# Another order of the events in a round of the wedge-score stage

## The reference

```python
Q = (Q_input @ Wq_w.T + Wq_b).reshape(b, sq, H, dk).transpose(0, 2, 1, 3)
Kh = K.reshape(b, sk, H, dk).transpose(0, 2, 1, 3)        # K = V = the context
gen = x @ proj_w.T + proj_b                                # _psi, for Q and for K
A, Bg, Th = gen[..., 0:8], gen[..., 8:16], clip(gen[..., 16:24], -8, 8)
psi_real, psi_imag = A * exp(Th) + Bg * cos(Th), Bg * sin(Th)
...
gram = qn2[..., :, None] * kn2[..., None, :]
wedge = sqrt(max(gram - tensor**2 - spinor**2, 0) + 1e-6)
hodge = sqrt(qn2 + 1e-6)[..., :, None] * sqrt(kn2 + 1e-6)[..., None, :]
scores = (geo_w[0]*wedge + geo_w[1]*tensor + geo_w[2]*spinor + geo_w[3]*hodge) / 4 / temperature
out = softmax(scores) @ Vh  -> reshape -> @ Wo_w.T + Wo_b
```

## Time and profile before

| | |
|---|---|
| median of 3 runs | 3064.28 us (3058.69 to 3073.77) |
| profiled execution: time, span | 3060.05 us, 3058.3 us |
| busy share of the span: TensorE, VectorE, ScalarE, GpSimd | 83%, 54%, 45%, 10% |
| mean granted clock of TensorE | 0.905 |
| the stage psi | about 2148 to 2782 us of the span |

### The profile page before, as it was taken

The page is one execution under the profiler, slowest core; times in us unless marked ns, Lnnn a source line. Parts: engine busy times, 40 slices in busy tenths (PEclk is TensorE's granted clock), DMA queues, the critical chain, the costliest instruction groups (busy, mean ns, idle before and its releaser), DMA issues. The chain is left out here.

```text
span 3058.3 us, 31620 instructions
## 1 busy us (share of the span) xinstructions
PE 2547.7 (83%) x11456; PEld 1497.1 (49%) x11456; DVE 1638.0 (54%) x3416; ACT 1386.3 (45%) x1989; POOL 319.9 (10%) x299
## 2 busy tenths in 40 slices
PE   5888888875888888879997688897588888887998
PEld 3555556552333333355454455565344445444555
DVE  4566555624666666716444587877555555541222
ACT  2333333311655555532222656553377777772221
POOL 0010001000000000000276000000211111000000
PEclk7899888967999998979898799998799999998999
DMA  2000000005333332240146221211300001001000
GB/s 72 7 14 14 14 14 14 7 7 153 57 65 63 63 64 55 46 150 0 35 72 104 94 70 42 84 42 42 101 7 28 28 28 35 14 14 62 14 21 21
DMA packets 113394, 140.81 MB, mean 46 GB/s; under 512 B 22004, under 2 KB 96004, under 8 KB 113240
## 3 DMA queue, kind: packets, MB, share of 16 engines
q1 hardware_dynamic: 98888, 123.97, 14.9%
q0 software_dynamic: 11904, 14.69, 3.0%
q10 hardware_dynamic: 2448, 0.14, 0.1%
HBM read 77.89 MB, written 35.39 MB: 37 GB/s over the span
## 5 line engine op out<-in xcount | busy, mean ns | idle before, releaser
L950 DVE TENSOR_REDUCE xattn_tops<-region 128x2 f32<-128x1024 f32 x256 | 306.3, 1220 | 126.0 <-PE region L734 125.9
L887 ACT ACTIVATE xattn_probs<-region 128x1024 f32<-128x1024 f32 x256 | 256.4, 1022 | 125.8 <-PE region L723 124.5
L2088 PE MATMUL region<-psi_fT 128*128 128x512 f32 x512 | 247.2, 622 | 24.7 <-DVE psi_low L2364 15.2
L122 PE MATMUL region<-gla_xT,weights_even 128*128 128x512 f32 (+1 forms) x416 | 206.4, 649 | 30.6 <-ACT gla_xT L214 30.6
L723 PE MATMUL region<-xattn_qs,xattn_ks 49*128 49x512 f32 x512 | 126.4, 495 | 61.8 <-DVE xattn_tops L950 31.4
L122 PE MATMUL region<-mamba_xT,weights_odd 128*128 128x512 f32 x320 | 157.6, 641 | 3.2 <-DVE mamba_xh L1927 3.2
L2088 PEld LDWEIGHTS region<-psi_fT 128*128 128x128 f32 x512 | 93.8, 196 | 135.2 <-issue 101.9
L122 PEld LDWEIGHTS region<-gla_xT,weights_even 128*128 128x128 f32 (+1 forms) x416 | 78.0, 196 | 144.5 <-issue 109.5
L131 PE MATMUL region<-weights_even,gla_work 128*128 128x256 f32 x512 | 123.4, 403 | 26.0 <-ACT gla_work L484 24.7
L752 PE MATMUL region<-xattn_probs,xattn_va 128*32 128x512 f32 x1024 | 141.8, 621 | 1.1 <-ACT xattn_o_T L914 1.1
L734 PE MATMUL region<-xattn_ks,xattn_qs 48*128 48x512 f32 x512 | 125.3, 488 | 13.9 <-DMA xattn_ks<-xattn_khi 9.5
(11 more groups left out here) (501 smaller groups left out, 5223.1 us busy)
## 6 DMA issues: line engine op xcount, KB each, us to landing
weights_even<-mamba_cs SPq DMA_DIRECT2D x32, 512.0 KB, 4.7
xattn_qs<-xattn_qhi SPq DMA_DIRECT2D x128, 64.0 KB, 2.3
xattn_ks<-xattn_khi SPq DMA_DIRECT2D x128, 64.0 KB, 2.3
moe_sums<-moe_picked SPq DMA_DIRECT2D x9, 512.0 KB, 8.6
gla_x<-in_x SPq DMA_DIRECT2D x8, 512.0 KB, 3.8
x_after_gla<-gla_res SPq DMA_DIRECT2D x8, 512.0 KB, 2.9
xattn_x<-x_after_gla SPq DMA_DIRECT2D x8, 512.0 KB, 4.1
xattn_ctxT<-in_ctxT SPq DMA_DIRECT2D x8, 512.0 KB, 4.4
```

The source lines that it names most:

```text
L122: last = st.nc.tensor.matmul(o[0:m, i, :], w[:, c, col + i * P:col + i * P + m], rhs[:, c, :], start=c == 0, stop=c == kc - 1)
L887: A_(probs[:, p % 3, a, :, :], st.region(f"k{v}")[:], ACT.Exp).then_inc(st.emptying(f"k{v}"), 1)
L950: V.tensor_reduce(tops[:, n % 2, t, a::2], st.region(f"q{u}")[:], AX, ALU.max).then_inc(st.emptying(f"q{u}"), 1)
L2088: last = mm(o[:, a, :], fT[:, h, 0, t * P:t * P + P], fT[:, h, 1 + a, :], start=True, stop=True)
```

## The change

The list of one round is written out event by event, and its order is another. No instruction is added, removed or changed. On each engine:

- **TensorE**: pv 0 goes ahead of score 1. Spread goes right behind score 2, ahead of turn 4. xT goes behind turn 5, and turn 6 right behind xT, ahead of score 5. Turn 7 goes behind score 8. At the end of a round the turns 0 to 3 and the products fT 1 to 3 alternate: fT 0, turn 0, fT 1, turn 1, turn 2, fT 2, turn 3, fT 3.
- **ScalarE**: the same moves for spread, xT and the turns 4 to 7. Growth comes behind the first head's exponentials, the sine ahead of the copies of fT 3.
- **VectorE**: features 4 comes behind the combine of score 7 instead of that of score 6, and the norm comes ahead of the copies of turns 0 and 1.
- The event `"score", b, 16` comes behind exp 1 instead of ahead of exp 0. VectorE has no work between the two places, so its own order there is as before.
- **GpSimd** and **SyncE** meet their events in the same order as before.

Since claims rotate, the moves also pair other events on a region.

```diff
@@ -2001,48 +2001,64 @@ def order(): for b in range(-2, B + 1):
-                for i in range(GQ):
-                    yield "score", b, i
-                    if i == 0:
-                        yield "sums", b - 1, 0
-                    if i == 1:
-                        yield "pv", b - 1, 0
-                    if i in (2, 4, 6, 7):
-                        yield "turn", b - 1, (2, 4, 6, 7).index(i) + 4
-                    if i == 3:
-                        yield "spread", b - 1, 0
-                    if i == 10:
-                        yield "pv", b - 1, 1
-                    if i in (9, 12):
-                        yield "scaled", b - 1, i // 12
-                    if i in (0, 1, 3, 5, 7, 9, 10):
-                        yield "features", b + 1, (0, 1, 3, 5, 7, 9, 10).index(i)
-                    if i == 3:
-                        yield "xT", b + 2, 0
-                    if i == 8:
-                        yield "Q", b + 2, 0
-                    if i == 11:
-                        yield "gen", b + 2, 0
-                    if i >= 12:
-                        yield "angles", b + 2, i - 12
-                yield "score", b, GQ
+                yield "score", b, 0
+                yield "sums", b - 1, 0
+                yield "features", b + 1, 0
+                yield "pv", b - 1, 0
+                yield "score", b, 1
+                yield "features", b + 1, 1
+                yield "score", b, 2
+                yield "spread", b - 1, 0
+                yield "turn", b - 1, 4
+                yield "score", b, 3
+                yield "features", b + 1, 2
+                yield "score", b, 4
+                yield "turn", b - 1, 5
+                yield "xT", b + 2, 0
+                yield "turn", b - 1, 6
+                yield "score", b, 5
+                yield "features", b + 1, 3
+                yield "score", b, 6
+                yield "score", b, 7
+                yield "score", b, 8
+                yield "turn", b - 1, 7
+                yield "features", b + 1, 4
+                yield "Q", b + 2, 0
+                yield "score", b, 9
+                yield "scaled", b - 1, 0
+                yield "features", b + 1, 5
+                yield "score", b, 10
+                yield "pv", b - 1, 1
+                yield "features", b + 1, 6
+                yield "score", b, 11
+                yield "gen", b + 2, 0
+                yield "score", b, 12
+                yield "scaled", b - 1, 1
+                yield "angles", b + 2, 0
+                yield "score", b, 13
+                yield "angles", b + 2, 1
+                yield "score", b, 14
+                yield "angles", b + 2, 2
+                yield "score", b, 15
+                yield "angles", b + 2, 3
+                yield "exp", b, 0
                 yield "growth", b + 2, 0
-                yield "exp", b, 0
                 yield "out", b - 1, 0
                 yield "fT", b + 1, 0
                 yield "exp", b, 1
+                yield "score", b, 16
                 yield "residual", b - 1, 0
+                yield "norm", b - 1, 0
                 yield "turn", b, 0
-                yield "turn", b, 1
-                yield "norm", b - 1, 0
                 yield "fT", b + 1, 1
                 yield "exp", b, 2
+                yield "turn", b, 1
                 yield "turn", b, 2
-                yield "turn", b, 3
                 yield "fT", b + 1, 2
                 yield "exp", b, 3
+                yield "turn", b, 3
+                yield "sin", b + 2, 0
                 yield "fT", b + 1, 3
-                yield "sin", b + 2, 0
```

## The result

Five runs of the changed kernel have a median of 3038.32 us (3035.92 to 3044.45), against 3064.28 of the kernel before (3056.21 to 3073.77, five runs). The ratio is 0.9916, 95% interval 0.9888 to 0.9944: faster by 0.8%, more than the 0.5% that can be told. Predicted were 3044 and a range of 3035 to 3057.

The account below looks back on a forecast made before the run. It took ScalarE to bound the seam and TensorE the stretch, in turns. Terms 8.0 + 1.1 + 1.2 + 1.5 + 5.5 + 3.0 = 20.3 us, from the median 3064.28, gave 3044, range 3035 to 3057.

Parts of the forecast that it names:

- The seam: From the last square root of one round to the first of the next: ScalarE is full, so 24.8 us stay.
- The stretch: TensorE's work from score 2 to the output product: 1.6 us less in each of rounds 1 to 5, 8.0 in all.
- score 7's wait: In the stretch, TensorE's 1.47 us wait for VectorE's combine of score 5, queued behind features 3, was to go.
- the new wait before turn 6: In the stretch, turn 6 claims score 4's region and was to wait 0.8 us for its combine.
- features 3 runs on VectorE from 30.6 to 34.1: Step in the stretch: features 3 ends before score 5's combine at 35.0 to 35.8, 0.9 before score 8 needs it.
- Round 6: Round without xT, Q or gen: pv 1 was to start earlier, gaining 1.1 us (0.8 to 1.3).
- The clock's cover: At four seams, slack of 1.6 us behind pv 0 and score 1 hides slow matmuls: 5.5 us (0 to 6.05).
- Round 7 and the tail: Round 7: score 2 freed earlier, 1.2 us. Last seam: inverted sums' product earlier by 3.0 us.
- Round 0: Score 8's 2.29 us wait shrinks as score 5's combine ends some 1.0 earlier: 1.5 us taken (0 to 2.7).
- The norm: Ahead of all pT copies on VectorE: score 0 at 80.85 instead of 80.67, hidden by ScalarE's 24.8 us seam.
- A moved wait: Rival: the wait before turn 6 comes out as 2.4 us and the stretch gains nothing: 3053 us, chance 0.19.
- More falls of the clock: Rival: alternating turns and fT products stop TensorE more often, two falls per round: 3077 us, chance 0.05.

Follow-up runs that it names:

- u_stretch: The kernel after, with the old order between score 1 and Q (spread, turns 4 to 7, xT, features 4); stage 619.32 us against 612.01.
- o_pv0: The kernel before, with pv 0 ahead of score 1 and nothing else; stage 626.51 us against 631.75.
- u_pv0_sin: The kernel after, with pv 0 back behind score 1 and the sine back behind the copies of fT 3; stage 624.53 us against 612.01.
- o_norm_alt: The kernel before, with the norm ahead of the copies of turns 0 to 3 and turns and fT products alternating; stage 626.29 us against 631.75.
- o_norm: The kernel before, with the norm ahead of the copies of turns 0 and 1 and nothing else; stage 641.64 us against 631.75.
- u_sin: The kernel after, with the sine back behind the copies of fT 3 on ScalarE; stage 614.77 us against 612.01.
- u_norm: The kernel after, with the norm back behind the copy of turn 1; stage 614.84 us against 612.01.
- u_pv0: The kernel after, with pv 0 back behind score 1; stage 636.24 us against 612.01.
- bias_at_q: The kernel after, with GpSimd's bias sum on x moved from xT to Q; stage 609.52 us against 612.01.
- o_stretch: The kernel before, with the new order between score 1 and Q alone; stage 627.97 us against 631.75.

## Why the prediction was right

Step by step, in the stage's terms (measured, then forecast):

- **The seam** stays ScalarE's: right, 24.75 for 24.8. Growth, exponential and sine changed places at no cost there (for the sine shown by putting it back, for growth by the unchanged length alone). The prediction missed that the sine's new place delays fT 3's copies and is free only because score 1 no longer stands ahead of pv 0. It cost nothing in the sum, but it is the largest interaction of the change: putting pv 0 back costs 24.2 us with the sine in its new place and 9.8 with it in the old one.
- **The stretch**, rounds 1 to 5: 5 x 1.19 = 6.0 for 8.0 (71.07 to 69.88 in rounds 3 and 5). The mechanism was right: score 7's wait, its end, the new wait before turn 6 (0.54 for 0.8). The term was too large by 0.4 a round. The step at fault is "features 3 runs on VectorE from 30.6 to 34.1": its first operation took 2 us longer beside GpSimd's sum, and score 5's combine came late again. Moving that sum gave back 0.27; the rest are some 0.1 us between events that the walk left out.
- **Round 6**: the order between score 1 and Q is worth 1.5 there for 1.1 (62.85 in u_stretch against 61.34).
- **The clock's cover**: rounds 1, 2 and 4 gained 1.96, 1.34 and 1.28 beyond the 1.19, and round 6 0.9 (63.77 to 62.86 in o_pv0): 5.5 for 5.5. Round 1's 1.96 is not pv 0's: with pv 0 behind score 1 it is there too (69.90 in u_pv0_sin), and o_pv0 has 73.84. It comes from the alternation of turns and fT products, which splits the wait of 4.01 us before the first sums' product into 1.90 and 1.19 (round 1 is 71.07 in o_norm_alt and 73.34 in o_norm, which lacks it). The prediction had this move as a danger only. That pv 0's place does the rest is shown by o_pv0, with rounds 2 to 5 all at 71.06 or 71.07 (before, rounds 2 and 4 were 72.41 and 72.35), and by u_pv0_sin against u_sin, 71.3 to 71.5 against 69.9.
- **How the clock's cover works** is another than forecast, so that the number is met to a tenth is luck. The prediction had slow matmuls behind the sums hidden by 1.6 us of slack. The slack was 1.10, and in the trace of after no low stretch begins behind the sums; of the slack at most 0.23 was used. Slow matmuls stopped coming there when the 1.13 us of wait before score 1 had gone. Why the clock falls at one seam and not at the next stays open. The prediction also counted four seams with a fall before the change and left out a fifth, 6-7 (granted clock 0.50 over 2686.8 to 2690.1, ahead of the sums).
- **Round 7 and the tail**: 3.58 + 0.86 = 4.4 for 1.2 + 3.0, which were both forecast ahead of the last inversion. There it is 3.58 for 4.2: by single moves 1.8 for the seam (o_pv0), 2.0 for the norm (u_norm, for 3.0) and 0.8 to 1.0 lost to the new order of the stretch (u_stretch); the rest stays open. The 0.86 behind the inversion is the clock's doing in this one trace, where pv 0 takes 5.35 us instead of 6.14; the last sums' product waits 2.55 us instead of 6.60 (compare).

```profile
2726.68 0.28 PE L2132 MATMUL region<-ident,psi_recip 128*16 128x128 f32 x1 [2.55 <-DVE psi_recip L2398]
2726.99 5.35 PE L2127 MATMUL region<-psi_pT,psi_ctxv 128*64 128x512 f32 x16
```

- **Round 0**: 2.35 for 1.5, and for half the reason. It takes the sine's place and the stretch's order together; either put back loses nearly all of it (112.99 and 113.20, against 113.18 before). The combine is 0.7 of it for the forecast 1.0 (score 8's wait of 2.44 in u_stretch is 1.71 after); the rest is the clock.
- **The norm**: "all this is hidden" was right for the kernel after, and wrong as a statement on the norm. Alone it costs 10 us. The prediction's walk has the fT products ready ahead of ScalarE's need, so that the late turns are free; it did not see that with the norm ahead and no alternation score 0 runs early, and did not ask what the longer wait behind it does to the clock.
- **The rivals.** A moved wait: it moved, at a third of the size. More falls of the clock: the granted clock fell at six of the seven seams in the trace of after (0-1, 2-3 to 6-7), against five before. The Trainium skill (TensorE: Matmul & The Clock Gate, "A second HAM failure mode: psum-queue depth-cycling") has the swings of the clock lower the throughput. The trace agrees on the swings; the loss did not come, because in these seams every fall lay ahead of the sums or ended within 1.0 us behind their inversion. The two runs that lost time (u_pv0 and o_norm) are this rival, with a new wait put in or the waits joined.

The parts add up to 19.7 for 20.3, but not each by itself: the stretch was 2.0 too large (rounds 1 to 5), round 0 0.85, round 6 0.4 and round 7 with the tail 0.2 too small. That the sum is met to 0.6 us owes something to luck.

So does the whole time. The measured median lies 5.7 under the forecast one, and from median to median 26.0 us were gained, the sum of all the prediction's high bounds (25.9). The stage accounts for 19.7 of it. In the two profiles another 4.1 stand ahead of the stage, whose start moved by up to 34 us from run to run, and 0.3 behind it.

## What to carry to other kernels

When all engines follow one written order and PSUM regions rotate, a move changes which reader each claim waits for; walk the claims with the measured durations, all the way round the ring, before judging a move by itself. Ask where an engine's unavoidable waits stand, and not only how long they are: here the same low clock cost nothing ahead of a wait that could shrink and up to 2.9 us behind the last one, and moving ready work (pv 0) into the place of a 1.13 us wait, and splitting a wait of 4.0 us, kept it from the costly place. Parts of such an order are not additive: the norm ahead, alone, lost 10 us, and all the other moves without pv 0 ahead lost 4.5 against the kernel before, so test moves in pairs; and measure on the stage, when layers ahead of it wander by more than the change is worth.

## What the runs showed of the hardware

- **A wait in one piece was followed by 1.2 GHz each time, the same wait in two was not.** A wait of 3.51 us stands in round 0 of all seven kernels with the sine behind fT 3's copies by ScalarE (before, the four o_ kernels, u_sin, u_pv0_sin), one of 3.62 or 3.63 in seams 2-3 to 5-6 of o_norm. Split into 1.57 and 1.67 in round 0 (after, u_pv0, u_norm, u_stretch, bias_at_q) the granted clock stayed at 1.00. In seam 0-1 the wait of 4.0 us before the sums' product (before, o_pv0, o_stretch, o_norm) was followed by 0.50, and its pieces of 1.90 and 1.19 in the other ten kernels by 1.00 (in u_pv0 until its wait of 3.07). In round 0:

```profile
2209.70:2215.00 5.30, 5.21 (x12) 2.99 (x13) 5.16 (x16) 3.12 (x5) 2.91 (x2) 0.50 0.00 0
```

```profile
2205.70:2211.00 5.30, 3.93 (x10) 1.65 (x11) 5.16 (x16) 3.16 (x5) 2.91 (x2) 1.00 0.00 0
```

(the kernel before, then the kernel after, at the same place). In the seams it fell at waits of at most 2.3 us as well, at some and not at others, and behind a wait of 2.55 or 2.56 in the last seam it was 0.50 in bias_at_q and 1.00 in u_stretch, so this is no bound.

- **VectorE stands still beside GpSimd.** L2317 sums two SBUF tensors of 128x896; it takes 1.09 us alone. With GpSimd's sum on x running from 2418.17 to 2420.54 it took from 2418.40 to 2421.48, which is the end of that sum and 0.94 more: it waited, it was not slowed in proportion. In round 0 of the kernel after a product (L2288), 0.69 us alone, took 2.73 beside the same sum. The Trainium skill (SBUF — State Buffer, "Who interferes with whom") says that a VectorE instruction with two SBUF inputs contends with a GpSimd instruction that reads SBUF, and that the port pair they share is an exclusive lock. The trace agrees.
